# A recurrent-attention kernel: two convolution banks exchanged, the gates in two pieces, and a subtraction put ahead of the third convolution

## The reference

```python
q, k, v = (causal_dwconv(x @ W, cw, cb) for each of q, k, v)   # 4 taps per channel, bias, SiLU
q, k = l2norm(rope(q)), l2norm(rope(k))                        # over each head
beta  = sigmoid(x @ bw + bb)                                   # per token and head
alpha = exp(-exp(A_log) * softplus(x @ gkw + gkb + dt_bias))
# over the tokens: o = q.S + D (q.k) v ;  S = alpha (S - beta k (k.S)) + beta k v
o = (x @ Wg) * silu(o * rsqrt(mean(o*o) + eps) * onorm_w)
s = o @ Wo
```

## Time and profile before

| | |
|---|---|
| median of 3 runs | 4372.28 us (4367.95 to 4373.02) |
| the profiled execution | 4367.48 us, of it a span of 4365.7 us |
| mean granted clock of TensorE over the span | 0.932 of full speed |
| PE busy | 3951.9 us, 91% of the span |
| DVE busy | 2911.1 us, 67% |
| ACT busy | 1871.6 us, 43% |
| POOL busy | 1581.5 us, 36% |

### The profile page before, as it was taken

How to read it: one execution, slowest core, us unless ns; L and a number is a source line. 1 busy time by engine, 2 the same in 40 slices (tenths; PEclk the granted TensorE clock), 3 DMA queues, 4 the chain that set the end, 5 groups by cost and what they waited for, 6 DMA issues and landing times.

```text
span 4365.7 us, 88936 instructions
## 1 busy us (share of the span) xinstructions
PE 3951.9 (91%) x31336; PEld 2670.1 (61%) x31336; DVE 2911.1 (67%) x6250; ACT 1871.6 (43%) x3972; POOL 1581.5 (36%) x1422
## 2 busy tenths in 40 slices
PE   5999999999999999578998998989989988989987
PEld 4555555555555555256766766767767766767675
DVE  3666666665656666488786877867867768768751
ACT  2444444443444444245444444444435435445431
POOL 2111111111111111146564655645555555646542
PEclk9999999999999999789898998998988899989976
DMA  2000000000000000211111111111111111111110
GB/s 103 1 16 1 16 1 16 1 16 1 16 1 16 1 16 1 74 30 25 30 21 36 32 20 47 25 38 24 33 38 20 32 39 28 24 36 32 20 39 6
DMA packets 299140, 105.72 MB, mean 24 GB/s; under 512 B 273265, under 2 KB 286833, under 8 KB 297841
## 3 DMA queue, kind: packets, MB, share of 16 engines
q1 hardware_dynamic: 298624, 99.24, 9.7%
HBM read 73.78 MB, written 25.95 MB: 23 GB/s over the span
## 4 chain that ended last, share of the span: by engine, by line
PE 37%; DVE 11%; issue 5%; ACT 4%; POOL 1%; DMA 0%; SPq 0%; DVEq 0%; POOLq 0%; ACTq 0%
PE d_ps L1855 6%; DVE d_acc L1522 4%; PE d_ps L2034 3%; PE d_ps L2049 3%; PE d_ps L1929 3%; PE d_ps L2068 3%; PE d_ps L1891 2%; PE d_ps L1944 2%; PE d_ps L1956 2%; PE d_ps L1833 2%; PE d_ps L1982 1%; PE d_ps L1908 1%; PE d_ps L1900 1%; PE d_ps L1870 1%; ACT d_acc L1292 1%
## 5 line engine op out<-in xcount | busy, mean ns | idle before, releaser
L231 POOL TENSOR_TENSOR f_qk<-f_m 128x512 f32<-128x512 f32 x128 | 162.3, 1273 | 1391.7 <-DVE f_m L416 1391.7
L1522 DVE SCALAR_TENSOR_TENSOR d_acc<-d_ps,d_cw,d_acc 128x511 f32<-128x511 f32 (+2 forms) x576 | 428.5, 744 | 116.3 <-ACT d_acc L1292 100.5
L1855 PE MATMUL d_ps<-d_xnT,d_wqkv 128*128 128x512 f32 x768 | 404.1, 653 | 0.5 <-DVE d_acc L1522 0.5
L316 ACT ACTIVATE f_pr<-f_sm,f_nb,f_qsc 128x256 f32<-128x256 f32 (+1 forms) x512 | 289.2, 566 | 160.8 <-DVE f_nb L453 158.9
L715 PE MATMUL f_ps<-f_m,f_w 128*128 128x512 f32 (+1 forms) x768 | 338.0, 594 | 14.5 <-DVE f_m L497 14.5
L1292 ACT ACTIVATE d_acc<-d_ps,d_cw 128x512 f32<-128x512 f32 x192 | 148.4, 774 | 350.1 <-PE d_ps L1855 349.2
L1159 POOL TENSOR_TENSOR d_qk<-d_m 128x512 f32<-128x512 f32 x128 | 162.1, 1266 | 302.5 <-DVE d_m L1533 297.3
L447 DVE CUSTOM_DVE_ANT_0 f_sm<-f_ps,f_mask 128x256 f32<-128x256 f32 (+1 forms) x512 | 179.8, 387 | 135.1 <-PE f_ps L621 129.5
L1164 POOL TENSOR_TENSOR d_rn<-d_ss,d_mhalf 128x8 f32<-128x8 f32 x128 | 221.0, 1726 | 127.8 <-DVE d_ss L1543 124.3
L715 PEld LDWEIGHTS f_ps<-f_m,f_w 128*128 128x128 f32 (+1 forms) x768 | 134.1, 178 | 214.7 <-issue 210.9
L646 PE MATMUL f_ps<-f_v,f_pT 128*128 128x64 f32 x1792 | 237.1, 273 | 19.3 <-DVE f_pT L461 19.3
(11 more groups left out here) (211 smaller groups left out, 9426.3 us busy)
## 6 DMA issues: line engine op xcount, KB each, us to landing
d_wqkv<-in_dwqkv SPq DMA_DIRECT2D x33, 768.0 KB, 4.6
blocks_scratch<-d_LT SPq DMA_DIRECT2D x128, 64.0 KB, 2.0
d_T<-inverse_scratch SPq DMA_DIRECT2D x128, 64.0 KB, 2.2
f_xin<-in_x SPq DMA_DIRECT2D x9, 512.0 KB, 4.3
d_xnT<-xnT_scratch SPq DMA_DIRECT2D x9, 512.0 KB, 6.5
xnT_scratch<-f_xT SPq DMA_DIRECT2D x8, 512.0 KB, 3.5
gate_scratch<-f_gate SPq DMA_DIRECT2D x8, 512.0 KB, 2.9
d_xnG<-xnT_scratch SPq DMA_DIRECT2D x8, 512.0 KB, 5.3
```

The costliest lines, as they stand in the source:

```text
L316: nc.scalar.activation(pr[:, u % AHEAD, j, k0:], sm[:, u % AHEAD, j, k0:], ACT.Exp, bias=nb[:, u % AHEAD, j:j + 1], scale=qsc[:, 0, w, h:h ...
L1522: V.scalar_tensor_tensor(out=a[:, k:], in0=ps[:, CV_BANK[n], 0:T - k], scalar=cw[:, X, s * CT + t, TAPS - 1 - k:TAPS - k], in1=a[:, k:], o ...
L1855: last = mm(ps[:, CV_BANK[n], :], wqkv[:, X, k, t * P:(t + 1) * P], xnT[:, k, :], start=k == 0, stop=k == KC - 1)
```

## The change

The banks of items 4 and 5 of the convolution are exchanged: item 4 now uses bank 2 and item 5 bank 4. Item 4's projection therefore waits for three items done, `solve` in the next turn for five and not six, and the key transposes (L1908, bank 4) for six and not five. VectorE's `gates` is cut after the two additions; the rest becomes `gates_mid`. In the tail VectorE makes the subtraction and transpose of the 16-row join ahead of item 2 of the convolution, then `gates_mid`, then items 2 and 3, and `gates_end` behind them. ScalarE and TensorE move the gates behind item 3 as well.

```diff
-CV_BANK = (3, 4, 2, 3, 4, 2)
+CV_BANK = (3, 4, 2, 3, 2, 4)
...
 # ScalarE, tail
             if conv:
                 first_tap(i, s, 2)
+                first_tap(i, s, 3)
+                silu(i, 2)
             if gated is not None:
                 gates_end(gated)
-            if conv:
-                first_tap(i, s, 3)
-                silu(i, 2)
...
 # VectorE, gates
             V.tensor_tensor(zg[:, :, H:], zg[:, :, H:], ...).then_inc(zg_rdy, 1)
+
+        def gates_mid(nb):
             dve.wait_ge(zg_rdy, 1 + 2 * nb + 2)
-
             dve.wait_ge(eb_rdy, 1 + nb + 1)
...
 # VectorE, tail
             if sub:
                 substitute(sub[0])
-            if conv:
-                conv_items(i, s, range(2, 3))
             if mid:
                 merge16_end(mid[0])
             if gated is not None:
-                gates_end(gated)
+                gates_mid(gated)
+            if conv:
+                conv_items(i, s, range(2, 3))
             if conv:
                 conv_items(i, s, range(3, 4))
+            if gated is not None:
+                gates_end(gated)
...
 # TensorE, conv / keys_T / carried
-                pe.wait_ge(cv_acc, 1 + val(i, 6, n - 2))
+                pe.wait_ge(cv_acc, 1 + val(i, 6, 3 if n == 4 else n - 2))
...
-                pe.wait_ge(cv_acc, 1 + val(i, 6, 5))
+                pe.wait_ge(cv_acc, 1 + val(i, 6, 6))
...
-                pe.wait_ge(cv_acc, 1 + val(min(i + 2, B * NG - 1) if isinstance(i, int) else i + 2, 6, 6))
+                pe.wait_ge(cv_acc, 1 + val(min(i + 2, B * NG - 1) if isinstance(i, int) else i + 2, 6, 5))
...
 # TensorE, tail
+            if conv_g:
+                conv(*conv_g, 3)
             if gated is not None:
                 gate_sums(gated)
-            if conv_g:
-                conv(*conv_g, 3)
```

More of the change, by code:

```diff
@@ L1716, in _ @@
         gates(0)
+        gates_mid(0)
         gates_end(0)
```

## The result

| | median | lowest to highest | runs |
|---|---|---|---|
| before | 4372.4 us | 4367.95 to 4373.02 | 4 |
| changed | 4295.14 us | 4288.39 to 4314.61 | 4 |

The ratio is 0.9836, with a 95% interval of 0.9818 to 0.9853: 77 us faster, where 71 were predicted. The profiled execution took 4295.77 us, its span 4294.0 us, and the mean granted clock rose from 0.932 to 0.940. From line 1810 on, a line of the changed kernel has a number 3 higher than before: L1817 is now L1820, L1855 L1858, L1956 L1959, L1966 L1969, L1982 L1985, L2034 L2037, L2060 L2063. The lines of VectorE and ScalarE that the text names keep their numbers.

What follows compares the result with a forecast made beforehand. TensorE bounds the kernel, so only its waits and its clock below full can be won. 17.4 + 21.4 + 32.2 + 3.5 - 3.5 = 71 us from 4372.28 gives 4301 us; range 4258 to 4345.

Steps and rivals of the forecast that it cites:

- The wait at the 32-row join, and the clock behind it: Plain turns: subtraction ahead of item 2 removes TensorE's wait, 17.4 us, and low-clock stretches in seven of 15 turns, 21.4 us.
- the rival that the clock doesn't come back: Plain turns: the wait goes but 1.2 GHz stretches fall elsewhere as often; gain 50 us, time 4322, chance 0.14.
- The 0.15 us a turn that was taken off for `out_heads`: Plain turns: item 2 and the Y32 copies end later, so TensorE may wait at `out_heads`; 0.15 us deducted per turn.
- The gate turns: Gates in two pieces let L1644 and L1956 come earlier; 4.6 us gained in each of seven turns, 32.2 us.
- the new wait at `gate_sums`: Gate turns: TensorE newly waits about 1.2 us at L1817 for `la` from VectorE's middle piece.
- the one of 1 us at `out_heads`: Gate turns: TensorE has a second new wait, about 1 us, for the Y32 copies of ScalarE.
- The half-clock stretch that was charged to these turns: Gate turns: the new waits bring a 1.2 GHz stretch costing 3.05 us, about 0.9 of it hidden; 2.2 deducted per turn.
- this rival: Gate turns: GpSimd holds up the middle piece, `la` 1.8 us later; 13 us less, gain 58, time 4314, chance 0.12.
- The banks: Start of turns: `solve` no longer waits for item 6; 0.15 us in each of 23 turns, 3.5 us, bounds 0 and 9.2.
- the lag: Start of turns: `solve` assumed to follow ScalarE's copies into Rf with the same lag as VectorE, leaving about 0.15 us.
- Output turns: Items 2 and 3 and the additions L1982 waits for end later; loss 0.5 us in seven turns, 3.5 us.
- this give-back: Output turns: GpSimd's copies start 0.9 us earlier, which may return part of the up to 1.1 us delay.

Runs made afterwards that it cites:

- e2: The kernel before with only the subtraction and transpose of the 16-row join moved ahead of convolution item 2: 4317.76 us, ratio 0.9885.
- e3: The changed kernel with the old banks and item 2 ahead of the subtraction again, so the gates' split and move alone: 4350.67 us, ratio 0.9959.
- e4: The kernel before with the bank exchange and its three waits alone: 4366.15 us, ratio 0.9994.
- e7: The changed kernel with `gates_mid` ahead of the subtraction on VectorE: 4263.86 us, ratio 0.9743.
- e1: The changed kernel with the bank exchange alone undone, old banks and their three old waits: 4292.1 us, ratio 0.983.
- e5: The changed kernel, a turn's first `solve` waiting only for the first of ScalarE's two L1390 copies into Rf, the second awaited at the third chunk: 4268.68 us.
- e6: The changed kernel with the old banks and `solve` first waiting for only the first of ScalarE's two copies into Rf: 4280.95 us, ratio 0.9807.
- e8: The changed kernel with item 2 ahead of the subtraction again in output turns only: 4289.99 us, ratio 0.9821.
- e10: The changed kernel timed again without an edit, six runs: 4289.59 us, ratio 0.9825.

## Why the prediction was right

The total of 71 us against 77 is right in its two large steps, and the parts can be put beside the runs one by one.

**The wait at the 32-row join, and the clock behind it: right.** The plain turns gained 48.8 us where 38.8 stood for these two terms. TensorE idles 16.9 us less in them, where 17.4 was said, and is busy 31.9 us less for the same work, where 21.4 was said for the clock. e2 shows that the subtraction's new place alone does it. That the low clock came from this wait was the step with the wider bounds, 0 to 21.4, and the rival that the clock doesn't come back stood against it. The windows settle it: with the wait 7 of 15 are low and 11 of 15 in e3, without it 0 of 15 in the changed kernel and in e2. The 10 us beyond the two terms are busy time elsewhere in the plain turns, and may be scatter: e4, with the wait, is busy 17.4 us less there than the kernel before. The 0.15 us a turn that was taken off for `out_heads` didn't come either.

**The gate turns: right in mechanism, with luck in the size.** L1644 comes 41.9 us behind the start of its turn and not 48.15, 6.2 earlier where 5.5 were said, and 36.9 us were won where the term was 32.2. Of this 18.8 are idle time and 18.1 busy time at a fuller clock. The forecast's waits come to 17.6 us less, 33.0 less seven times 2.2, but by two misses that cancel: the new wait at `gate_sums` is 2.0 us, not 1.2, and the one of 1 us at `out_heads` didn't come. The half-clock stretch that was charged to these turns came in all seven. The middle piece is held up 0.9 us beside GpSimd; the rival had 1.8 for this and 13 us in all. Against it the prediction held that GpSimd's copies are short and have gaps; two of the three delays in the turn above end with such a copy. e7 puts the piece where GpSimd is idle: the wait goes, and 12 to 16 us come back in the gate turns, the clock behind the wait included. So this rival was half true inside a forecast that held. The Trainium skill, SBUF — State Buffer, section "SBUF: two separate sides", has a GpSimd instruction and a VectorE one in a two-port mode, or with two SBUF inputs where the GpSimd one reads SBUF, exclude each other for a whole instruction. The trace agrees for L1501, which has two such inputs and ends within 0.1 us behind a copy. L1496 and L1508 have one input and end so as well; whether they ran in a two-port mode no run here shows.

The split and the move alone don't make this term, as the expectation of e3 had it: they give 12.7 us in the gate turns, in part because `la` then stands behind item 2 (8 us of the difference of 24). Most of the term needs the subtraction and the middle piece ahead of item 2, as the prediction's working has them.

**The banks: the term of 3.5 us was too high, 0 to within the noise.** e1 and e4 show it from both sides. The step that failed is the lag: it took `solve` to follow ScalarE's copy as closely as VectorE's item 6, and so to be released by item 6. `solve` starts 0.40 us behind the copy, and 0.44 behind the first copy in e5, which takes 0.58 us from 2751.01 on; in e6, where item 6 does release it, it starts 0.13 behind that. So the copy was the later limit before the change as well, by some 0.1 us, and the wait was 1.50 us before and is 1.50 after, under the same label.

**Output turns: this step failed.** It said that the additions come later, because item 2 now starts behind the subtraction, and a wait that grows. The wait fell, from 7.8 to 4.3 us. The timeline of DVE before, and then after, in one output turn:

```profile
2921.55 2.32 DVE L1522 SCALAR_TENSOR_TENSOR d_acc<-d_ps,d_cw,d_acc 128x511 f32<-128x511 f32 x3 [0.30 <-ACT d_acc L1292]
2923.79 2.15 DVE L1658 COPY d_T<-d_kbg 32x512 f32<-32x512 f32 x2
2925.96 1.28 DVE L1714 TENSOR_TENSOR d_xio<-d_xio,d_ps 128x512 f32<-128x512 f32 x2
```
```profile
2884.60 0.69 DVE L1649 TENSOR_TENSOR d_kbg<-d_T,d_ps 128x512 f32<-128x512 f32 x1 [4.13 <-PE d_ps L1959]
...
2885.96 4.50 DVE L1522 SCALAR_TENSOR_TENSOR d_acc<-d_ps,d_cw,d_acc 128x511 f32<-128x511 f32 x6
2890.37 0.85 DVE L1658 COPY d_T<-d_kbg 32x512 f32<-32x512 f32 x2
2891.26 1.28 DVE L1714 TENSOR_TENSOR d_xio<-d_xio,d_ps 128x512 f32<-128x512 f32 x2
```

Items 2 and 3 do end later, but GpSimd's copies now run beside the convolution, and VectorE's copies L1658 come behind them: 0.85 us in place of 2.15. Before, they started at 2923.79 beside GpSimd's last copy and the product L1149 behind it:

```profile
2923.76 0.61 POOL L1223 COPY d_Rf<-d_R 32x512 f32<-32x512 f32 x1 [0.17 <-POOL d_Rf L1223]
2924.62 1.04 POOL L1149 TENSOR_TENSOR d_lm<-d_tri,d_la 128x512 f32<-128x512 f32 x1 [0.25 <-POOL d_Rf L1223]
```

After, the last of GpSimd's four copies starts at 2888.54 and ends at 2889.15. The step had this give-back as a possibility and set it below the loss; it is above it. e8 puts item 2 back and has the wait of 7.7 us again. Even so the seven turns sum to 6.9 us more. That is the clock: TensorE idles 7.2 us less in them and is busy 14.1 us more for the same work. One of them took 92.44 us where their median is 87.67. Windows of its first 15 us, and of the same part of another output turn, after:

```profile
3119.26:3134.30 15.04, 15.04 (x73) 12.18 (x74) 7.80 (x18) 6.26 (x14) 8.54 (x10) 0.50 0.15 21
2825.62:2840.70 15.08, 14.40 (x114) 12.15 (x114) 11.78 (x27) 8.05 (x19) 12.44 (x13) 0.89 0.16 23
```

Both turns begin behind a wait of some 1.5 us; one goes on at half clock for 15 us and the other doesn't. The sums of e10, 4.2 us above before, and of e4, with the old order, 4.0 above, speak for scatter and not for a cost of the change.

**What stays open.** e5 took 10.6 us of waiting from the starts of turns. Its profiled span is 10.9 us shorter than the changed kernel's first, but 0.7 longer than that of e10; and its median fell by 21 to 26 us, and e7's by more than its waits. The clock after the remaining waits could make the difference, and executions of one kernel scatter by it: the changed kernel's ten runs lie between 4273 and 4316 us. No run here separates the two.

## What to carry to other kernels

Price a wait of the bound engine twice: once for its length, and once for the clock that the windows behind it show. Here the wait of 19.6 us in plain turns was worth some 35 to 55 by the sums over these turns.

When a piece of work is moved on VectorE, look at what GpSimd does at the new time, instruction by instruction. The same move was worth 12 to 16 us more in the gate turns when the small instructions came before GpSimd's long product, and in the output turns copies moved behind GpSimd's paid for the delay.

Where two limits end within 0.1 or 0.2 us of each other, lifting one is worth next to nothing alone. Take the lag behind each engine from a wait that this engine surely ended: here 0.40 us behind ScalarE and 0.13 behind VectorE. The releaser that a trace names is then only a candidate; lift the other one and see.

## What the runs showed of the hardware that was not expected

Short waits of TensorE are followed by stretches at 1.2 GHz in part of the cases; in others the same wait of the same kernel is not. Behind the wait of about 1.2 to 1.4 us at the 32-row join 7 of 15 windows were low before and 11 of 15 in e3; behind one of 1.5 us at the start of a turn there were 15 us at 0.50 in one turn and 0.89 in another; behind the 2.0 us at `gate_sums` the clock fell in all seven turns. It doesn't look like mere chance either: before, and in e4, exactly one of the two plain turns of each iteration was low, in all seven iterations, though not always the same one. Why is not shown. So a kernel whose waits are short still scatters: the kernel before gave 4355.55 to 4382.53 us in 20 runs beside e1, and the changed kernel spread over 43 us.

Small VectorE instructions were held up beside GpSimd by more than their own length: L1496 took 0.59 us and not 0.20, L1508 0.49 and not 0.20, and two copies L1658 2.15 and not 0.85. Over all 64 copies the median is 747 ns before and 412 after. VectorE is busy 35 us less in the looped turns for the same instructions.
